# Edge loop of a graph-attention layer: a third PSUM buffer, one-bank softmax with key rows from DRAM, sums one place later, and values and counts in rows of 33

## The chip, the cores and the metric

The kernel runs on one core of one Trainium2 chip. The metric is the device time of one execution in microseconds (us). The granted clock is the share of TensorE's full 2.4 GHz that the records show. The engines are called PE (TensorE; PEld its weight loads), DVE (VectorE), ACT (ScalarE), POOL (GpSimd) and SP (the sync engine, which here only issues DMAs).

## The reference

`x` is 6,250 nodes of 256 features; there are 106,250 edges, sorted by their target `dst`, each with 256 features of its own. Eight heads of 32.

```python
x = x + gnn(layernorm(x), src, dst, edge_attr)      # first part
    q, k, v = x @ Wq + bq, x @ Wk + bk, x @ Wv + bv ; e = edge_attr @ We
    alpha = (q[dst] * (k[src] + e)).sum(head) / sqrt(32)          # per edge and head
    ea    = exp(alpha - segment_max(alpha, dst)[dst])
    out   = segment_sum((v[src] + e) * ea / segment_sum(ea, dst)[dst], dst) + x @ Ws + bs
x = x + ffn(layernorm(x))                            # second part: top 2 of 8 experts, 256 -> 512 -> 256
```

## The kernel before

Three phases follow one another. The first projects 49 tiles of 128 nodes to q, k, v and the skip term, writes a table of v and k rows to DRAM and prepares the tables of the edge loop. The second, the edge loop (lines 678 to 1162), is what the change is about. The third adds the skip term, normalises again and runs the experts.

**Items and chunks.** The edges are cut into 880 items of 128 edges (one per partition), each item belonging to one tile of 128 target nodes. Sixteen items are a chunk, so there are 55 chunks. A place is a step of a chunk, 0 to 15. The loop is written out in full: every engine runs its own list of steps, made by `plan`, and semaphores with credits (`counters`) keep the lists in step.

**One item.** PE turns the 128x256 edge features (`ps_t`, L960), ACT copies them to `aT` (L905), PE multiplies by `We` into the left half of a PSUM buffer `ps_e` (L976) and gathers the q rows into its right half by a one-hot matmul (L980). POOL has gathered the v and k rows of the edges' sources by an indirect DMA into `kv_ring` (L818, four slots). DVE adds e to both (L1059), reduces the item before over the heads (L1047) and multiplies k+e by q (L1065). There are two `ps_e` buffers: `project` of item i waits until DVE has multiplied item i-2.

**The softmax of a chunk, one chunk behind.** The 16 x 8 scores of a chunk lie side by side as 128 columns. POOL masks them (`am`, L835), PE turns them (`scores`, L1010), so that a partition is an (item, head) pair and DVE can scan along the edges for each target's running minimum, forwards and backwards (L1075, L1079). A target whose edges go on in the next item needs minima across partitions: PE spreads each partition's first and last key as rows (`keys`, L1004 to L1006), ACT makes "not the same key" distances from them (L926, L927), PE spreads the minima (L1014 to L1016), and DVE takes two fused add-and-minimum passes (`own`, L1084, L1088). DVE then forms and subtracts the least value (L1094 to L1101), PE turns the result back and forms the rescaling exponent (`turn_scores`, L1020 to L1023), and ACT exponentiates (L942 into the eight count columns of `ve_ke`, L945 into `factor`), which releases `ea_ready`.

**Weighing and summing, up to two chunks behind.** POOL multiplies the 256 values of an item by their eight weights (`weigh`, L828), ACT makes a one-hot of the targets (`select`, L883, L887), PE sums by target (L1029 into one of two `ps_u` buffers) and DVE adds the sum to the node tile's slot (L1135). At the start of a chunk DVE rescales the slot in use by `factor` (L1113 for 256 values, L1114 for 8 counts). `LAG` says how many places behind the scores each of these runs: weigh 15 (POOL runs about four places ahead of DVE), select 11, sum and add 13.

**SP** issues, in one list, the loads of edge features (`a_ring`, four slots), of target rows (`loc_c`) and of the chunk's tables (`run_c`, `resets`, `tab_c`). In the first phase it issues the stores of each node tile, and ahead of tile 43's stores a block of first loads for the edge loop (`edge_loop_inputs`).

Of the kernel before, what the change touches and what calls it, by code (L numbers as in the profile page):

```python
# [6 lines left out]
F32 = mybir.dt.float32  # L7
# [7 lines left out]
P = 128  # L15
# [6 lines left out]
N_KV = 4  # L22
N_A = 4
# [8 lines left out]
def gnn_ffn(nc, x, src, dst, edge_attr, Wq, bq, Wk, bk, Wv, bv, We, Ws, bs, Wg, bg, gbias, W1, b1, W2, b2, out):  # L32
# [23 lines left out]
    with ExitStack() as ctx:  # L56
# [29 lines left out]
        reset_table = dram("reset_table", (IT, P))  # L86
        loc_table = dram("loc_table", (NCH * CH // SEL, SEL * P), BF16)
# [26 lines left out]
        values, counts = node_slots[:, 0:NT, 0:D], node_slots[:, 0:NT, D:UW]  # L114
# [17 lines left out]
        run_c = [sb(f"run_c{i}", [P, P], F32, c_soft) for i in range(2)]  # L132
        resets = [sb(f"resets{i}", [P, P + 1], F32, c_soft) for i in range(2)]
# [3 lines left out]
        reset_loaded = [sem(f"reset_loaded{i}", c_soft) for i in range(2)]  # L137
        loc_loaded = [sem(f"loc_loaded{i}", c_soft) for i in range(NLOC)]
# [13 lines left out]
        with ExitStack() as c1:  # L152
# [21 lines left out]
            head_i = sb1("head_i", [P, 1], I32)  # L174
            stepped = sb1("stepped", [NT, IT])
# [54 lines left out]
            tables_written = sem("tables_written", c1)  # L230
            resets_ready = sem("resets_ready", c1)
# [29 lines left out]
            def _(sp):  # L261
# [26 lines left out]

                def to_table(table, tile):
                    sp.dma_start(table[0:nf * P, :].rearrange("(b p) e -> p b e", p=P), tile[:, 0:nf, :]).then_inc(tables_written, 16)  # L290
                    if n_last:
                        sp.dma_start(table[nf * P:IT, :], tile[0:n_last, nf, :]).then_inc(tables_written, 16)

                def edge_loop_inputs():
# [4 lines left out]
                    sp.wait_ge(tables_written, 16 * (1 + 3 * (2 if n_last else 1)))  # L299
                    sp.dma_start(tab_c[:, 0, :, :].rearrange("p t i -> p (t i)"), tab_table[:, 0:3 * CH]).then_inc(tab_loaded[0], 16)  # L300
                    sp.dma_start(run_c[0][:, :], run_table[0:CH, :][:, None, :].to_broadcast([CH, H, P])).then_inc(run_loaded[0], 16)
                    sp.dma_start(resets[0][:, 0:P], reset_table[0:CH, :][:, None, :].to_broadcast([CH, H, P])).then_inc(reset_loaded[0], 16)
                    for n in range(NLOC - 1):
                        sp.dma_start(loc_c[n][:, :], loc_table[n:n + 1, :].to_broadcast([P, SEL * P])).then_inc(loc_loaded[n], 16)

                for j in range(NT):
# [8 lines left out]
                    if j == LOCS_OUT:  # L315
                        sp.wait_ge(tables_ready, LOCS)
# [10 lines left out]
                sp.wait_ge(tables_written, 16 * (1 + 3 * (2 if n_last else 1)))  # L327
# [126 lines left out]
            def _(dve):  # L454
# [223 lines left out]
        with ExitStack() as c3:  # L678
# [12 lines left out]
            ve_ke = sb3("ve_ke", [P, 2 * CH + 2, UW])  # L691
            sel = sb3("sel", [P, N_W, P])
# [5 lines left out]
            key_prev = sb3("key_prev", [P, 1])  # L698
# [9 lines left out]
            ps_e = [ps3(f"ps_e{i}", [P, 512]) for i in range(2)]  # L708
# [3 lines left out]
            ps_a, ps_k = ps_ak[:, 0:P], ps_ak[:, P:P + KW]  # L712
            ps_r, ps_x, ps_d = ps_rx[:, 0:KW], ps_rx[:, KW:KW + P], ps_rx[:, KW + P:KW + P + H]


            s, at, grant = counters(c3, a_turned=N_A, aT_ready=2, e_ready=2, ve_added=N_KV, kq_ready=2,
                                    alpha_ready=0, apart_ready=0, sel_ready=0, apartT_ready=0, selT_ready=0, weighted=2 * CH, summed=2 * CH, acc_added=2,

                                    am_ready=0, run_by_head=0, keyed=0, keys_apart=0, key_kept=0, offs_ready=0,
                                    scores_turned=0, scanned_f=0, scanned=0, min_spread=0, owned_f=0, owned=0, least1_ready=0,  # L720
                                    least_ready=0, shifted_ready=0, shifted_turned=1, ea_ready=0, rescaled=2, values_rescaled=0,
# [47 lines left out]
            def _(sp):  # L769
# [13 lines left out]
                def load(c, par, steps):  # L783
                    for kind, i, back in steps:
# [7 lines left out]
                        if i == 0 and c > 0:  # L792
# [4 lines left out]
                                         ).then_inc(reset_loaded[par], 16)  # L797
                        if c * CH + i < N_A:
# [8 lines left out]
            def _(pool):  # L807
# [14 lines left out]
                def weigh(c, par, i):  # L822
# [4 lines left out]
                    ve = by_head(ve_ke[:, par * CH + i, 0:D], C)  # L827
                    g.tensor_tensor(ve, ve, ve_ke[:, par * CH + i, D:UW][:, :, None].to_broadcast([P, H, C]),  # L828
# [27 lines left out]
            def _(act):  # L856
# [40 lines left out]
                def emit(c, par, steps):  # L897
                    for kind, i, back in steps:
# [19 lines left out]
                        elif kind == "apart":  # L918
# [3 lines left out]
                            act.wait_ge(s["keyed"], at("keyed", c - 1))  # L922
# [3 lines left out]
                            nc.scalar.activation(not_f[:, :], ps_k, ACT.Abs, scale=-1.0, bias=run[:, 0:1])  # L926
                            nc.scalar.activation(not_l[:, :], ps_k, ACT.Abs, scale=-1.0, bias=run[:, P - 1:P]).then_inc(s["keys_apart"], 1)  # L927
                            nc.scalar.copy(key_prev[:, :], run[:, P - 1:P]).then_inc(s["key_kept"], 1)
# [7 lines left out]
                        elif kind == "exp":  # L936
# [5 lines left out]
                            nc.scalar.activation(ve_ke[:, (1 - par) * CH:(2 - par) * CH, D:UW], by_head(ps_x, H), ACT.Exp, scale=-SCALE)  # L942
# [5 lines left out]
                over_chunks(act, emit, what="select", parts={3: "apart", 4: "offs", 11: "exp"})  # L948

            @block.tensor  # L950
            def _(pe):
# [18 lines left out]
                def project(c, i, n):  # L970
                    pe.wait_ge(s["aT_ready"], at("aT_ready", c * CH + i))

                    pe.wait_ge(s["ve_added"], at("ve_added", c * CH + (i - 2)))
                    pe.wait_ge(s["kq_ready"], at("kq_ready", c * CH + (i - 2)))
# [828 lines left out]
```

## Time and profile before

| | |
|---|---|
| median of 3 runs | 2530.81 us (2526.67 to 2532.15) |
| the profiled execution, its time | 2519.88 us |
| its span, first to last instruction | 2518.1 us |
| first phase | to about 222 us |
| edge loop: first and last matmul with `We` begin | 227.5 us, 1903.5 us |
| mean granted TensorE clock | 0.967; 1.00 from 500 to 1500 us |

Busy time counts overlapping records of an engine once. The ends of matmuls are modelled, so a stall of PE shorter than a matmul's modelled tail doesn't show as idle time; it shows as a longer distance between starts.

### The profile page before, as it was taken

The page shows a single profiled execution, that of the slowest core. Times are in us where ns is not written, and L with a number is a line of the kernel's source. Part 1 is how long each engine was busy: PE and PEld are TensorE (multiplying, and loading weights), DVE is VectorE, ACT ScalarE, POOL GpSimd, SP SyncE. Part 2 cuts the span into 40 slices and gives each one's busy share as a digit, 9 for nine tenths or more (in the row PEclk, how much of TensorE's full clock was granted, in tenths as well). Part 3 has the DMA queues.
Part 4 walks back from the last instruction along what each step waited for, and adds up shares of the span by engine and source line. Part 5 has one row for each costly group of instructions (what it writes and reads, how often), then busy time and mean ns, then how long its engine had stood idle before and what let it go on. Part 6 is the DMA issues. An engine that isn't in the chain of part 4 may idle for free. (4 is left out here: it accounts for less than half of the span.)

```text
span 2518.1 us, 62222 instructions
## 1 busy us (share of the span) xinstructions
PE 2368.8 (94%) x13314; PEld 1994.0 (79%) x13315; DVE 1990.4 (79%) x5253; ACT 1573.8 (62%) x4349; POOL 1809.0 (72%) x2137
## 2 busy tenths in 40 slices
PE   6998999999999999999999999999995658999998
PEld 2445888888888888888888888888883647999998
DVE  6875999999999999999999999999997872222222
ACT  1122677777777777777777777777774125666665
POOL 4223788888888888888888888888886205666666
PEclk9999999999999999999999999999998558999999
DMA  7325877788788778778877777777772672433443
GB/s 230 129 107 182 243 230 229 227 233 232 225 232 228 222 231 232 230 230 232 233 230 229 232 223 231 233 226 227 232 229 81 193 224 53 71 63 63 69 67 54
DMA packets 337730, 476.37 MB, mean 189 GB/s; under 512 B 61382, under 2 KB 268556, under 8 KB 337116
## 3 DMA queue, kind: packets, MB, share of 16 engines
q0 software_dynamic: 92576, 259.72, 39.2%
q1 hardware_dynamic: 238556, 213.23, 27.7%
q8 instruction: 102, 1.67, 0.3%
q14 instruction: 208, 1.70, 0.2%
q10 hardware_dynamic: 6288, 0.05, 0.2%
HBM read 425.40 MB, written 50.57 MB: 189 GB/s over the span
## 5 line engine op out<-in xcount | busy, mean ns | idle before, releaser
L818 POOL DMA_INDIRECT kv_ring<-vk_table,tab_c x880 | 859.7, 977 | 250.9 <-issue 168.2
L976 PE MATMUL ps_e<-we_sb,aT 128*128 128x256 f32 x3520 | 916.4, 383 | 12.3 <-DVE ve_ke L1065 7.8
L976 PEld LDWEIGHTS ps_e<-we_sb,aT 128*128 128x128 f32 x3520 | 600.6, 191 | 82.7 <-issue 31.3
L1059 DVE TENSOR_TENSOR ve_ke<-kv_ring,ps_e 128x512 f32<-128x512 f32 x880 | 601.4, 683 | 47.9 <-PE ps_e L980 17.9
L828 POOL TENSOR_TENSOR ve_ke<-ve_ke 128x256 f32<-128x256 f32 x880 | 551.2, 630 | 16.9 <-ACT factor L945 3.3
L1029 PE MATMUL ps_u<-ve_ke,sel 128*128 128x264 f32 x1760 | 544.3, 391 | 10.1 <-DVE node_slots L1135 5.6
L980 PE MATMUL ps_e<-q_slots,selT 128*128 x1760 | 517.2, 375 | 0.0
L905 ACT COPY aT<-ps_t 128x256 f32<-128x256 f32 x880 | 325.4, 370 | 283.6 <-PE ps_t L960 246.9
L1135 DVE TENSOR_TENSOR node_slots<-node_slots,ps_u 128x264 f32 x880 | 369.9, 420 | 29.0 <-PE ps_u L1029 25.0
L980 PEld LDWEIGHTS ps_e<-q_slots,selT 128*128 128x128 f32 x1760 | 334.7, 190 | 45.6
L1047 DVE TENSOR_REDUCE alpha<-ve_ke 128x8 f32<-128x256 f32 x880 | 362.9, 412 | 2.0
L1065 DVE TENSOR_TENSOR ve_ke<-ve_ke,ps_e 128x256 f32<-128x256 f32 x880 | 361.6, 411 | 1.9
L883 ACT ACTIVATE apart<-iota_free,tab_c 128x128 f32<-128x128 f32 x880 | 348.2, 396 | 3.5 <-PE ps_u L1029 3.2
L960 PE MATMUL ps_t<-ident,a_ring 128*128 128x128 f32 x1760 | 336.4, 273 | 7.1 <-issue 7.1
L887 ACT ACTIVATE sel<-apart 128x128 f32<-128x128 f32 x880 | 272.9, 310 | 105.4 <-ACT apart L883 2.8
L960 PEld LDWEIGHTS ps_t<-ident,a_ring 128*128 128x128 f32 x1760 | 247.0, 141 | 105.3 <-issue 8.1
L1029 PEld LDWEIGHTS ps_u<-ve_ke,sel 128*128 128x128 f32 x1760 | 270.0, 190 | 32.9 <-POOL ve_ke L828 22.6
L1764 DVE TENSOR_TENSOR y_full<-ps_y,b_sb 128x256 f32<-128x256 f32 x112 | 47.6, 425 | 278.4 <-PE ps_y L1733 278.4
L1725 PE MATMUL ps_h<-tT,w_now 128*128 128x128 f32 x1792 | 219.6, 276 | 0.0
L1641 POOL DMA_INDIRECT t_in<-xn_table,take_i x112 | 111.0, 991 | 149.9 <-DVE gate_of L1760 88.6
L1733 PE MATMUL ps_y<-w_sb,hT 128*128 x896 | 212.0, 379 | 0.0
L1725 PEld LDWEIGHTS ps_h<-tT,w_now 128*128 128x128 f32 x1792 | 210.3, 193 | 0.1
(255 smaller groups left out, 2631.3 us busy)
## 6 DMA issues: line engine op xcount, KB each, us to landing
a_ring<-in_edge_attr SPq DMA_DIRECT2D x880, 128.0 KB
loc_c<-loc_table SPq DMA_DIRECT2D x220, 128.0 KB, 3.9
kv_ring<-vk_table,tab_c POOLq DMA_INDIRECT x880
vk_table<-kv_out SPq DMA_DIRECT2D x49, 256.0 KB, 2.0
skip_table<-skip_out SPq DMA_DIRECT2D x49, 128.0 KB, 1.7
skip<-skip_table SPq DMA_DIRECT2D x7, 896.0 KB, 9.5
xn_table<-node_slots SPq DMA_DIRECT2D x7, 896.0 KB, 5.1
w_sb<-in_L_ffn_W SPq DMA_DIRECT2D x2, 2048.0 KB, 10.1
```

Of the source, the lines that this page charges most:

```text
L818: g.indirect_dma_start(out=kv_ring[:, i % N_KV, :], out_offset=None, in_=vk_table, in_offset=bass.IndirectOffsetOnAxis(ap=tab_c[:, c % N_T ...
L828: g.tensor_tensor(ve, ve, ve_ke[:, par * CH + i, D:UW][:, :, None].to_broadcast([P, H, C]), ALU.mult).then_inc(s["weighted"], 1)
L883: nc.scalar.activation(apart[i % 2][:, :], iota_free[:, :], ACT.Abs, scale=-1.0, bias=tab_c[:, c % N_TAB, 1, i:i + 1]).then_inc(s["apart_r ...
L960: last = t.transpose(ps_t[i % 2][:, k * P:(k + 1) * P], a_ring[:, i % N_A, k * P:(k + 1) * P], ident[:, :])
L976: t.matmul(ps_e[i % 2][:, 0:D], aT[i % 2][:, k * P:(k + 1) * P], we_sb[:, k, :], start=(k == 0), stop=(k == KD - 1))
L980: last = t.matmul(ps_e[i % 2][:, D:2 * D], selT[i // SEL % 2][:, i % SEL * P:(i % SEL + 1) * P], q_moving[part][:, bass.ds(n * SLOT, D)], ...
L1029: t.matmul(ps_u[i % 2][:, 0:UW], sel[:, i % N_W, :], ve_ke[:, (par + back) % 2 * CH + i, :], start=True, stop=True).then_inc(s["summed"], 1)
L1047: v.tensor_reduce(alpha[par][:, i * H:(i + 1) * H], by_head(ve_ke[:, 2 * CH + i % 2, 0:D], C), AX_X, ALU.add).then_inc(s["alpha_ready"], 1)
L1059: v.tensor_tensor(ve_ke[:, to:ke + 1:ke - to, 0:D], kv.rearrange("p (t d) -> p t d", t=2), e[:, None, :].to_broadcast([P, 2, D]), ALU.add) ...
L1065: v.tensor_tensor(ve_ke[:, ke, 0:D], ve_ke[:, ke, 0:D], ps_e[i % 2][:, D:2 * D], ALU.mult).then_inc(s["kq_ready"], 1)
L1135: v.tensor_tensor(to, sofar, ps_u[i % 2][:, 0:UW], ALU.add).then_inc(s["acc_added"], 1)
L1725: last = t.matmul(ps_h[par][:, f * P:(f + 1) * P], w1_now[par][:, k, f * P:(f + 1) * P], tT[par][:, k * P:(k + 1) * P], start=(k == 0), st ...
```

## The change

1. **Three `ps_e` buffers** in place of two (`N_E = 3`, buffer by item number modulo 3): `project` of item i waits for DVE's item i-3.
2. **The softmax in one bank.** `ps_ak` and `ps_rx` become `ps_s`: the turned scores (and later, in the same columns, the turned-back result), the spread minima, and the exponent. The third `ps_e` takes the bank that this frees.
3. **Key rows from DRAM.** The three spreading transposes of `keys`, and ACT's copy of the key carried to the next chunk, go away. The first phase writes two tables of keys (five more DMA issues at tile 9, rows of 32 bytes), and SP loads two rows per chunk, spread over the partitions (two more DMAs per chunk).
4. **One spread minimum by 8 columns**: the transpose of the carried minimum (L1014) becomes a matmul of 8 columns.
5. **Places.** sum and add 14, select 12; PE's scores at place 4 (was 3), minima 7 (6), turn_scores 12 (10); ACT's exp 13 (11). DVE's `least` is split over places 7 and 8, the subtraction moves from 8 to 9.
6. **Rows of 33.** `ve_ke` and the node slots hold, for each head, 32 values and then the count, where they held 256 values and then 8 counts. Every operation on values or counts now goes through rows of 32 at a pitch of 33; the rescaling is one operation over 264.

```diff
+N_E = 3
-        values, counts = node_slots[:, 0:NT, 0:D], node_slots[:, 0:NT, D:UW]
+        by_tile = node_slots[:, 0:NT, 0:UW].rearrange("p j (h w) -> p j h w", w=C + 1)
+        sums, counts = by_tile[:, :, :, 0:C], by_tile[:, :, :, C]
...
+            def load_keys(sp, c):
+                keys = key_c[c % 2]
+                sp.dma_start(keys[:, 0:P], first_table[c * CH:(c + 1) * CH, :].rearrange("(o i) h -> o (i h)", o=1).to_broadcast([P, P])
+                             ).then_inc(key_loaded[c % 2], 16)
+                sp.dma_start(keys[:, P:KW], last_table[c * CH:(c + 1) * CH + 1, :].rearrange("(o i) h -> o (i h)", o=1).to_broadcast([P, P + H])
+                             ).then_inc(key_loaded[c % 2], 16)
...
+                def keys_to_tables():
+                    sp.wait_ge(keys_ready, 3)
+                    sp.dma_start(last_table[0:1, :], no_key[:, :]).then_inc(tables_written, 16)
+                    for k, table in enumerate((first_table[0:IT, :], last_table[1:IT + 1, :])):
+                        sp.dma_start(table[0:nf * P, :].rearrange("(b p) h -> p b h", p=P), keys_io[:, k, 0:nf, :]).then_inc(tables_written, 16)
+                        if n_last:
+                            sp.dma_start(table[nf * P:IT, :], keys_io[0:n_last, k, nf, :]).then_inc(tables_written, 16)
...   # edge_loop_inputs
+                    load_keys(sp, 0)
...   # SP, place 0 of each chunk, after run_c and resets
+                            if c >= 2:
+                                sp.wait_ge(s["keys_apart"], at("keys_apart", c - 2))
+                            load_keys(sp, c)
...
+            ve_heads = ve_ke[:, :, :].rearrange("p s (h w) -> p s h w", w=C + 1)
-            ps_ak = ps3("ps_ak", [P, 512])
-            ps_rx = ps3("ps_rx", [P, 512])
+            ps_s = ps3("ps_s", [P, 512])
+            ps_a, ps_r, ps_d = ps_s[:, 0:P], ps_s[:, P:P + KW], ps_s[:, P + KW:P + KW + H]
+            ps_x = ps_a
...
-                       select=FIRST_WEIGH,
-                       sum=FIRST_WEIGH + 2,
-                       add=FIRST_WEIGH + 2)
+                       select=FIRST_WEIGH + 1,
+                       sum=FIRST_WEIGH + 3,
+                       add=FIRST_WEIGH + 3)
...   # POOL
-                    ve = by_head(ve_ke[:, par * CH + i, 0:D], C)
-                    g.tensor_tensor(ve, ve, ve_ke[:, par * CH + i, D:UW][:, :, None].to_broadcast([P, H, C]),
+                    ve = ve_heads[:, par * CH + i, :, 0:C]
+                    g.tensor_tensor(ve, ve, ve_heads[:, par * CH + i, :, C:C + 1].to_broadcast([P, H, C]),
...   # ACT
-                            act.wait_ge(s["keyed"], at("keyed", c - 1))
+                            act.wait_ge(key_loaded[1 - par], 32 * ((c - 1) // 2 + 1))
-                            nc.scalar.copy(key_prev[:, :], run[:, P - 1:P]).then_inc(s["key_kept"], 1)
-                over_chunks(act, emit, what="select", parts={3: "apart", 4: "offs", 11: "exp"})
+                over_chunks(act, emit, what="select", parts={3: "apart", 4: "offs", 13: "exp"})
...   # PE
-                    pe.wait_ge(s["kq_ready"], at("kq_ready", c * CH + (i - 2)))
+                    pe.wait_ge(s["kq_ready"], at("kq_ready", c * CH + (i - N_E)))
-                        elif kind == "keys":
...
-                            t.transpose(ps_r[:, KW - P:KW], min_l[par][:, 0:1].to_broadcast([P, P]), ident[:, :])
+                            t.matmul(ps_r[:, P:P + H], min_l[par][:, 0:1].to_broadcast([P, P]), ident[:, P - H:P], start=True, stop=True)
-                over_chunks(pe, emit, what="sum", parts={0: "keys", 3: "scores", 6: "minima", 10: "turn_scores"})
+                over_chunks(pe, emit, what="sum", parts={4: "scores", 7: "minima", 12: "turn_scores"})
...   # DVE
-                    v.tensor_tensor(ve_ke[:, to:ke + 1:ke - to, 0:D], kv.rearrange("p (t d) -> p t d", t=2),
-                                    e[:, None, :].to_broadcast([P, 2, D]), ALU.add).then_inc(s["ve_added"], 1)
+                    v.tensor_tensor(ve_heads[:, to:ke + 1:ke - to, :, 0:C], kv.rearrange("p (t h c) -> p t h c", t=2, c=C),
+                                    by_head(e, C)[:, None, :, :].to_broadcast([P, 2, H, C]), ALU.add).then_inc(s["ve_added"], 1)
...
-                    v.tensor_tensor(a, a, factor[:, :, None].to_broadcast([P, H, C]), ALU.mult).then_inc(s["values_rescaled"], 1)
-                    v.tensor_tensor(held, held, factor[:, :], ALU.mult).then_inc(s["rescaled"], 1)
+                    v.tensor_tensor(a, a, factor[:, :, None].to_broadcast([P, H, C + 1]), ALU.mult).then_inc(s["rescaled"], 1)
-                over_chunks(dve, emit, what="add", parts={3: "scan", 4: "scan_back", 6: "own", 7: "least", 8: "shift"})
+                over_chunks(dve, emit, what="add", parts={3: "scan", 4: "scan_back", 6: "own",
+                                                         7: "least_first", 8: "least_last", 9: "shift"})
```

## Rows read from the trace of the kernel before

**Rows 1.** The page, busy time, share of the span and instructions of each engine.

```profile
PE 2368.8 (94%) x13314; PEld 1994.0 (79%) x13315; DVE 1990.4 (79%) x5253; ACT 1573.8 (62%) x4349; POOL 1809.0 (72%) x2137
```

**Rows 2.** Windows: busy us of each engine, clock, DMA share, GB/s, inside the loop.

```profile
500.00:1000.00 500.00, 494.84 (x2810) 427.32 (x2809) 477.84 (x1225) 362.97 (x1050) 425.57 (x541) 1.00 0.80 229
```

**Rows 3.** Line L976 alone: durations in ns, first and last start.

```profile
L976 PE MATMUL ps_e<-we_sb,aT x3520: 378/379/797, 227.5 to 1903.5; 128*128 128x256 f32 x196
```

**Rows 4.** Timeline of PE over one chunk: start us, us, instruction.

```profile
988.55 0.27 PE L1004 MATMUL ps_ak<-ident,key_prev 128*128 128x128 f32 x1
...
988.87 0.61 PE L1029 MATMUL ps_u<-ve_ke,sel 128*128 128x264 f32 x2
...
991.30 1.03 PE L976 MATMUL ps_e<-we_sb,aT 128*128 128x256 f32 x4
...
993.07 1.03 PE L976 MATMUL ps_e<-we_sb,aT 128*128 128x256 f32 x4
...
994.40 0.71 PE L1029 MATMUL ps_u<-ve_ke,sel 128*128 128x264 f32 x2
...
995.17 1.03 PE L976 MATMUL ps_e<-we_sb,aT 128*128 128x256 f32 x4
...
1004.34 1.03 PE L976 MATMUL ps_e<-we_sb,aT 128*128 128x256 f32 x4
...
1006.32 1.10 PE L976 MATMUL ps_e<-we_sb,aT 128*128 128x256 f32 x4
...
1007.50 0.28 PE L1020 MATMUL ps_rx<-ident,min_f 128*128 128x8 f32 x2
...
1008.01 0.61 PE L1029 MATMUL ps_u<-ve_ke,sel 128*128 128x264 f32 x2
...
1017.99 0.45 PE L976 MATMUL ps_e<-we_sb,aT 128*128 128x256 f32 x1 [0.32 <-DVE ve_ke L1065]
```

**Rows 5.** Timeline of DVE, same chunk, places 8 to 10.

```profile
1005.77 0.41 DVE L1065 TENSOR_TENSOR ve_ke<-ve_ke,ps_e 128x256 f32<-128x256 f32 x1
...
1006.63 0.68 DVE L1059 TENSOR_TENSOR ve_ke<-kv_ring,ps_e 128x512 f32<-128x512 f32 x1
...
1008.23 0.68 DVE L1059 TENSOR_TENSOR ve_ke<-kv_ring,ps_e 128x512 f32<-128x512 f32 x1
```

**Rows 6.** Timeline of POOL, same chunk.

```profile
993.37 0.41 POOL L835 TENSOR_TENSOR am<-tab_c,alpha 128x128 f32<-128x128 f32 x1
993.74 1.18 POOL L828 TENSOR_TENSOR ve_ke<-ve_ke 128x256 f32<-128x256 f32 x2
...
998.71 0.98 POOL L818 DMA_INDIRECT kv_ring<-vk_table,tab_c  x1 [0.16 <-issue]
...
1000.49 0.98 POOL L818 DMA_INDIRECT kv_ring<-vk_table,tab_c  x1 [0.16 <-issue]
...
1010.86 0.63 POOL L828 TENSOR_TENSOR ve_ke<-ve_ke 128x256 f32<-128x256 f32 x1
```

**Rows 7.** Timeline of ACT, same chunk: the exponent that releases the weighing.

```profile
1008.47 0.26 ACT L945 ACTIVATE factor<-ps_rx,carried 128x8 f32<-128x8 f32 x1
```

**Rows 8.** Waits from 300 to 1900 us, PE's longest and SP's longest: us, times, longest.

```profile
PE ps_e L976 <- DVE ve_ke L1065: 5.5, 21, 0.7
...
SPq L802 <- PE ps_t L960: 487.7, 790, 3.7
```

**Rows 9.** Single lines: operations on rows with gaps (min/median/max ns); the counts' rescaling.

```profile
L559 DVE TENSOR_TENSOR tab<-t_rep,ii_i x1: 1061/1061/1061, 110.9 to 110.9; 128x880 f32<-128x880 f32 x1
L360 POOL TENSOR_TENSOR dst_sb<-run_g x1: 1665/1665/1665, 53.1 to 53.1; 128x889 f32<-128x889 f32 x1
L1114 DVE TENSOR_TENSOR node_slots<-node_slots,factor 128x8 f32 x55 | 11.5, 209 | 0.0
```

**Rows 10.** Timeline of SP and DVE at the end of the first phase.

```profile
203.15 0.62 SPq L301 DMA_DIRECT2D run_c<-run_table  x1
...
210.09 0.69 DVE L615 TENSOR_TENSOR kv_out<-ps_p,b 128x512 f32<-128x512 f32 x1 [5.40 <-DMA skip_table<-skip_out]
```

More of the change, by code:

```diff
@@ L113, in gnn_ffn @@
         x_sb = node_slots[:, 1:NT + 1, D:2 * D]
-        values, counts = node_slots[:, 0:NT, 0:D], node_slots[:, 0:NT, D:UW]
+        values = node_slots[:, 0:NT, 0:D]
+        by_tile = node_slots[:, 0:NT, 0:UW].rearrange("p j (h w) -> p j h w", w=C + 1)
+        sums, counts = by_tile[:, :, :, 0:C], by_tile[:, :, :, C]
         x1 = node_slots[:, 0:NT, UW:SLOT]
@@ L132, in gnn_ffn @@
         run_c = [sb(f"run_c{i}", [P, P], F32, c_soft) for i in range(2)]
+        KW = 2 * P + H
+        key_c = [sb(f"key_c{i}", [P, KW], F32, c_soft) for i in range(2)]
         resets = [sb(f"resets{i}", [P, P + 1], F32, c_soft) for i in range(2)]
@@ L137, in gnn_ffn @@
         reset_loaded = [sem(f"reset_loaded{i}", c_soft) for i in range(2)]
+        key_loaded = [sem(f"key_loaded{i}", c_soft) for i in range(2)]
         loc_loaded = [sem(f"loc_loaded{i}", c_soft) for i in range(NLOC)]
@@ L315, in _ @@
                     if j == LOCS_OUT:
+                        with nc.allow_non_contiguous_dma(reason="eight head keys of an item"):
+                            keys_to_tables()
                         sp.wait_ge(tables_ready, LOCS)
@@ L521, in floats @@
                         v.tensor_scalar(run_f, run_g[:, :, :], BIG, None, ALU.mult).then_inc(tables_ready, 1)
-                    else:
+                        v.memset(no_key[:, :], -BIG).then_inc(keys_ready, 1)
+                        then(v.tensor_scalar(head_row[:, :], iota_free[:, 0:H], BIG / H, None, ALU.mult))
+                    else:
+                        for k, e in enumerate((0, P - 1)):
+                            v.tensor_tensor(keys_io[:, k, :, :], run_f[:, :, e:e + 1].to_broadcast([P, IB, H]),
+                                            head_row[:, None, :].to_broadcast([P, IB, H]), ALU.add).then_inc(keys_ready, 1)
                         dve.wait_ge(gathered[1], 16 * IB)
@@ L925, in emit @@
                             act.sem_inc(s["act_pace"], 1)
-                            nc.scalar.activation(not_f[:, :], ps_k, ACT.Abs, scale=-1.0, bias=run[:, 0:1])
-                            nc.scalar.activation(not_l[:, :], ps_k, ACT.Abs, scale=-1.0, bias=run[:, P - 1:P]).then_inc(s["keys_apart"], 1)
-                            nc.scalar.copy(key_prev[:, :], run[:, P - 1:P]).then_inc(s["key_kept"], 1)
+                            nc.scalar.activation(not_f[:, :], key_c[1 - par][:, :], ACT.Abs, scale=-1.0, bias=run[:, 0:1])
+                            nc.scalar.activation(not_l[:, :], key_c[1 - par][:, :], ACT.Abs, scale=-1.0, bias=run[:, P - 1:P]
+                                                 ).then_inc(s["keys_apart"], 1)
                         elif kind == "offs":
@@ L941, in emit @@
                             act.sem_inc(s["act_pace"], 1)
-                            nc.scalar.activation(ve_ke[:, (1 - par) * CH:(2 - par) * CH, D:UW], by_head(ps_x, H), ACT.Exp, scale=-SCALE)
+                            nc.scalar.activation(ve_heads[:, (1 - par) * CH:(2 - par) * CH, :, C], by_head(ps_x, H), ACT.Exp, scale=-SCALE)
                             act.wait_ge(s["rescaled"], at("rescaled", c - 2))
@@ L979, in project @@
                     for part in range(2):
-                        last = t.matmul(ps_e[i % 2][:, D:2 * D], selT[i // SEL % 2][:, i % SEL * P:(i % SEL + 1) * P],
+                        last = t.matmul(ps_e[(c * CH + i) % N_E][:, D:2 * D], selT[i // SEL % 2][:, i % SEL * P:(i % SEL + 1) * P],
                                         q_moving[part][:, bass.ds(n * SLOT, D)], start=(part == 0), stop=(part == 1))
@@ L998, in emit @@
                                 next_tiles[:] = node_tiles_of(c + 1)
[L999 to L1006 removed]
                         elif kind == "scores":
                             pe.wait_ge(s["am_ready"], at("am_ready", c - 1))
[L1009 removed]
+                            pe.wait_ge(s["ea_ready"], at("ea_ready", c - 2))
                             t.transpose(ps_a, am[:, :], ident[:, :]).then_inc(s["scores_turned"], 1)
@@ L1089, in softmax @@
                                                op1=ALU.min, accum_out=min_l[1 - par][:, :]).then_inc(s["owned"], 1)
-                    elif part == "least":
+                    elif part == "least_first":
                         dve.wait_ge(s["offs_ready"], at("offs_ready", c - 1))
@@ L1095, in softmax @@
                                                op0=ALU.add, op1=ALU.min).then_inc(s["least1_ready"], 1)
+                    elif part == "least_last":
                         dve.wait_ge(s["least1_ready"], at("least1_ready", c - 1))
@@ L1261, in _ @@
                 for j, n in groups:
-                    nc.gpsimd.tensor_tensor(by_heads(x1[:, j:j + n, :]), by_heads(values[:, j:j + n, :]),
+                    nc.gpsimd.tensor_tensor(by_heads(x1[:, j:j + n, :]), sums[:, j:j + n, :, :],
                                             inv[:, j:j + n, :][:, :, :, None].to_broadcast([P, n, H, C]), ALU.mult).then_inc(att_ready, 1)
```

56 lines of the change are left out of this document (24 added, 32 removed).

## The prediction

> **What bounds the kernel now.** I read the page first, for the engines' shares of the whole span [rows 1], then the windows, for the stage that the change touches. From 500 to 1000 us PE is busy 99% of the time at full clock, DVE 95.6% and POOL 85% [rows 2]. So PE is the first suspect, with DVE right behind it. The reader is to see that busy time doesn't settle it: a PE record carries a modelled tail, so a short stall hides in it. The list of waits has PE waiting little: its longest entry is 5.5 us of 1600 [rows 8]. Starts of the same instruction tell more, so the third view is L976 alone: 880 items take from 227.5 to 1903.5 us, 1.906 us an item, 30.5 us a chunk of 16 [rows 3].
>
> The fourth view is PE's timeline over one chunk. An undisturbed place takes 993.07 - 991.30 = 1.77 us [rows 4], and 16 of them 28.3 us. The softmax's own PE work comes on top: three spreading transposes take 988.87 - 988.55 = 0.32 us, so 0.11 each; the turned scores 0.11; the three of `minima`, by the same price, 0.33; `turn_scores` 1008.01 - 1007.50 = 0.51 [rows 4]. Together 1.27, and 29.6 with the items. The other 30.5 - 29.6 = 0.9 us of a chunk is PE standing still, in short stalls.
>
> Where? Place 3 takes 995.17 - 993.07 = 2.10: 0.33 over 1.77, of which the scores explain 0.11. The sum starts at 994.40; half of POOL's pair of weighings that starts at 993.74 and takes 1.18 ends at about 994.33 [rows 4, 6]. PE waits for the item that POOL's mask has delayed. Place 9 takes 1006.32 - 1004.34 = 1.98, 0.21 too much: `project` of item 10 waits for DVE's L1065 of item 8, which starts at 1005.77 and takes 0.41, so ends at 1006.18 [rows 4, 5]. DVE was late because of the softmax passes at places 6 to 8. The wrap to the next chunk ends the same way: 0.32 us idle, released by L1065 [rows 4].
>
> The other engines' need of a chunk decides what can be won. DVE's undisturbed place takes 1008.23 - 1006.63 = 1.60 [rows 5]; with softmax and rescaling its busy share gives 0.956 x 30.5 = 29.1 us. POOL's place takes 1000.49 - 998.71 = 1.78, and the mask 993.74 - 993.37 = 0.37 more [rows 6]: 16 x 1.78 + 0.37 = 28.9 us. Three engines need 29.6, 29.1 and 28.9 us, and their coupling makes 30.5 of it.
>
> **The change, part by part.**
>
> *PE's instructions.* Dropping `keys` takes away 0.32 us. The carried minimum as an 8-column matmul is two passes for one transpose: `turn_scores` is four such passes and a transpose in 0.51, 0.10 each [rows 4], so it adds about 0.1 (between 0, if passes overlap as in a tail, and 0.11). Net -0.22 us a chunk; PE's need becomes 29.6 - 0.22 = 29.4 us.
>
> *PE's stalls, 0.9 us a chunk.* With three buffers, `project` of item 10 waits for item 7, which DVE multiplied a whole place (1.6 to 1.8 us) earlier than item 8; the 0.21 at place 9 and the 0.32 at the wrap are far under that, and go. With sums at lag 14 and the weighing still at 15, the item that the mask delays is wanted one place later, 1.77 us against a delay of 0.22; it goes too. What should stay are the irregular delays of whole chunks, and new small ones, since PE will lead DVE by only 29.4 against 29.1. I take two thirds of the 0.9, 0.6 us; the bounds are none of it and all of it.
>
> *DVE.* The rescaling loses the counts' operation, mean 0.209 us [rows 9], but it lay in the first one's completion time, so between 0 and 0.2 us. Splitting `least` fills a short wait; at most 0.1. Nothing is added to its loop.
>
> *Rows of 33.* The trace has no row with rows of 32 at a pitch of 33. The nearest on DVE writes rows of 16 at a pitch of 48: 880 elements in 1061 ns, 1.21 ns each with all overhead [rows 9], where the flat L1059 takes 0.68 us for 512, 1.33 each [rows 5]. So 0. On POOL the nearest has rows of 127 at a pitch of 128: 889 elements in 1665 ns, 1.87 ns each [rows 9], against 0.63 us for 256, 2.46 each, in the weighing [rows 6]. So 0 as well, but there the rows are long and only seven, and POOL has little room: 30.5 - 28.9 = 1.6 us a chunk, 0.1 us on each weighing of 0.63. That is the bound from above that turns the sign, and the rival below.
>
> *The moved steps.* `turn_scores` goes from place 10 to 12, 2 x 1.77 = 3.5 us later, and with it the exponent, for which POOL's first weighing waits, with every later gather behind it in POOL's list. Now the exponent ends at 1008.47 + 0.26 = 1008.73 and that weighing starts at 1010.86 [rows 6, 7]: 2.1 us of cover, so POOL would wait 1.4 us. PE wants the result one place (1.77 us) later than now, so PE has no loss from it; POOL loses 1.4 us only if it doesn't get them back where it now waits for DVE (30.5 - 28.9 = 1.6 us a chunk in all). I take 0, and 1.4 us as the bound. ACT waits at exp as now, for the same distance from `turn_scores`. DVE's subtraction one place later frees `run_c` a place later for SP, which then issues four loads of up to 0.62 us [rows 10] ahead of an edge-feature load; SP waits 487.7 us in 790 waits, 0.6 each [rows 8], and `a_ring` is four items, 7 us, deep. So 0.
>
> *Key loads.* Two rows of about 512 bytes to 128 partitions are 0.13 MB a chunk; at 229 GB/s a chunk moves 7.0 MB [rows 2], so 2% more on a DMA share of 0.80. Hidden. ACT's key copy goes; ACT is busy 73% [rows 2], so 0.
>
> *Once.* In the first phase the block of first loads on SP already makes DVE wait 5.40 us for a store [rows 10]; two more issues of up to 0.62 us each lengthen it by 1.2 us. The five table writes at tile 9, at the same price, are 3 us of SP between stores; SP has that much idle, so 0 to 3; I take 0.3. Together 1.5 us.
>
> *Sum.* 0.22 + 0.6 = 0.82 us on 54 full chunks is 44 us, less 1.5: 42 us. The profiled execution would go from 2519.88 to 2478 us. It lies 11 us below the median of the runs shown, 2530.81; on that scale the forecast is **2489 us**. The bounds of this case: with every stall gone, (0.22 + 0.9) x 54 - 1.5 = 59 us off, 2472; with half of the 0.6, (0.22 + 0.3) x 54 - 1.5 = 27 off, 2504.
>
> **The rivals.** *The wait only moves.* PE's `sum` still waits, through two `ps_u` buffers, for DVE's addition two items back. If PE's lead now ends there, or DVE waits at `scan` for scores that PE turns one place later, a chunk takes perhaps 30.1 us. For it: DVE's 29.1 leaves 0.3 us to PE's 29.4. Against: today no wait for an addition is long enough to head PE's list [rows 8], and DVE's peak of softmax work (places 6 to 8) is what the third buffer bridges. 0.4 x 54 - 1.5 = 20 us off: 2511.
>
> *The late exponent holds POOL.* If POOL can't use its slack elsewhere, its chunk is 28.9 + 1.4 = 30.3, and the change does next to nothing: 0.2 x 54 - 1.5 = 9 us off, 2522. Against it: the 1.6 us of present slack is larger than 1.4.
>
> *POOL pays for the rows: slower.* The weighing's 2.46 ns an element lie 0.59 above the 1.87 of the operation on long rows [rows 6, 9]. If that is what its factor, read anew every 32nd element, costs it, and gaps in the values' rows cost the same again, a weighing takes 256 x 0.59 ns = 0.15 us more, a chunk 28.9 + 16 x 0.15 = 31.3, and the loop (31.3 - 30.5) x 54 = 43 us more: 2575. It decides from 0.1 us a weighing, 16%, on. Against it: the difference may as well be an operation's fixed cost, which weighs more on 256 elements than on 889. The Trainium skill (GPSIMD Engine Reference, section Performance pitfalls for Q7 kernels) states that reads with a step over 8 bytes cost POOL about half as much again, and that it is the inner step that counts. Read so, it doesn't reach this operation, whose inner steps are 4 bytes and 0; if it did, an estimate by that page makes a weighing 0.95 us and the loop 189 us longer. No run here shows its price.
>
> **How the numbers follow.** Stalls mostly gone, 0.64; the wait only moves, 0.18; late exponent or nothing, 0.10; rows cost POOL or DVE, 0.08. For 8 in 10 the range takes the first two whole, with the 11 us between profile and median as play: 2466 to 2520. The measurement can tell about 0.2%, 5 us. Faster: 0.64 + 0.18 + 0.05 of the third case, 0.87; the same 0.05; slower 0.08.
>
> **What would show it.** Right: L976's starts span about 1676 - 44 = 1632 us; places 3 and 9 take 1.77 in PE's timeline (place 4 has the 0.11 of the scores); L828 stays at 0.62 to 0.63 and L1059 at 0.68; DVE's busy share rises to 98%; POOL's first weighing waits for ACT. Wrong: a longer L828; PE's starts 1.9 apart with `acc_added` as releaser; DVE idle at the scan; or a chunk that POOL's wait for the exponent sets.

## The result, and the profile after

The changed kernel takes 2536.8 us (median of 10 executions, 2533.6 to 2543.5) against 2527.7 us of the kernel before on the same chip (10, 2525.3 to 2533.1): ratio 1.0038, 95% interval 1.0030 to 1.0045. It is slightly slower, by more than measurement play. The forecast was 2489 us. The profiled execution took 2536.19 us, its span 2534.3.

The page's busy line and the window inside the loop, in the columns of [rows 1, 2]:

```profile
PE 2366.8 (93%) x13204; PEld 1993.9 (79%) x13205; DVE 1975.2 (78%) x5201; ACT 1570.8 (62%) x4294; POOL 1812.8 (72%) x2137
500.00:1000.00 500.00, 489.87 (x2752) 423.86 (x2751) 465.41 (x1195) 357.62 (x1020) 422.47 (x535) 1.00 0.79 232
```

PE and DVE do *less* of a window than before: no engine became full. `project`'s first matmul, now L1013, answers to [rows 3]:

```profile
L1013 PE MATMUL ps_e<-we_sb,aT x3520: 379/379/792, 230.6 to 1916.2; 128*128 128x256 f32 x196
```

It starts 3.1 us later than before and takes 1685.6 us instead of 1676, so a chunk of 16 is 1685.6 / 879 x 16 = 30.68 us against 30.51. In the chunk that starts at 1182.50 us the stalls named at place 3 and at the wrap are gone, that at place 9 is smaller (1.85 us against 1.98), and others stand in their place: places 1, 2, 6 and 8 take 1.96 to 2.02 us. The waits from 300 to 1900 us (us, times, longest), and below them SP's own queue:

```profile
POOL ve_ke L865 <- ACT factor L982: 48.1, 49, 1.3
PE ps_u L1057 <- DVE node_slots L1161: 15.3, 30, 2.5
PEld ps_t L997 <- DMA a_ring<-in_edge_attr: 5.1, 10, 1.2
...
SPq L839 <- PE ps_t L997: 370.1, 554, 3.7
SPq L828 <- DVEq L1132: 49.9, 52, 1.1
```

Two are new and come once a chunk: POOL's first weighing waits 1 us for the exponents, and SP's load of the run rows waits 1 us for DVE's shift. The timelines of one chunk show the first (DVE, PE, ACT, POOL in turn):

```profile
1016.89 0.28 DVE L1131 TENSOR_TENSOR least<-ps_s,least 128x128 f32<-128x128 f32 x1
...
1019.85 0.31 PE L1051 MATMUL ps_s<-ident,least 128*128 128x128 f32 x1
...
1020.28 0.41 ACT L979 ACTIVATE ve_ke<-ps_s 128x128 f32<-128x128 f32 x1 [0.70 <-PE ps_s L1051]
1020.47 0.24 ACT L982 ACTIVATE factor<-ps_s,carried 128x8 f32<-128x8 f32 x1
...
1018.89 0.97 POOL L855 DMA_INDIRECT kv_ring<-vk_table,tab_c  x1 [0.16 <-issue]
1020.90 0.62 POOL L865 TENSOR_TENSOR ve_ke<-ve_ke 128x256 f32<-128x256 f32 x1 [1.03 <-ACT factor L982]
1021.66 0.99 POOL L855 DMA_INDIRECT kv_ring<-vk_table,tab_c  x1
```

The shift has ended at 1017.17, but PE turns it at 1019.85, by its place in the list; the exponents end at 1020.71 and POOL, idle for 1.03 us, goes on at 1020.90. The gather behind it starts at 1021.66, 2.77 us after the one before; a place is 1.78 us [rows 6]. In [rows 6, 7] this weighing had 2.1 us to spare.

### The profile page after: what moved, and what is told of

The parts are those of the page before. It is cut to its first block and busy times, and to the rows that moved or that the text cites. A ratio compares the mean times of both kernels' runs of the same rounds, so it can differ in the third digit from the quotient of the medians.

```text
span 2534.3 us, 61900 instructions
## 1 busy us (share of the span) xinstructions
PE 2366.8 (93%) x13204; PEld 1993.9 (79%) x13205; DVE 1975.2 (78%) x5201; ACT 1570.8 (62%) x4294; POOL 1812.8 (72%) x2137
## 5 line engine op out<-in xcount | busy, mean ns | idle before, releaser
L1013 PE MATMUL ps_e<-we_sb,aT 128*128 128x256 f32 x3520 | 908.7, 381 | 2.0 <-ACT aT L942 1.3
L1087 DVE TENSOR_TENSOR ve_ke<-kv_ring,ps_e 128x512 f32<-128x512 f32 x880 | 600.1, 682 | 74.1 <-PE ps_e L1017 31.7
L1013 PEld LDWEIGHTS ps_e<-we_sb,aT 128*128 128x128 f32 x3520 | 601.7, 191 | 49.3 <-ACT aT L942 2.9
L1057 PE MATMUL ps_u<-ve_ke,sel 128*128 128x264 f32 x1760 | 561.0, 401 | 32.6 <-DVE node_slots L1161 20.9
L1161 DVE TENSOR_TENSOR node_slots<-node_slots,ps_u 128x264 f32 x880 | 370.2, 421 | 29.2 <-DVE node_slots L1141 15.5
```

The lines of the kernel that those rows point to most:

```text
L1013: t.matmul(ps_e[(c * CH + i) % N_E][:, 0:D], aT[i % 2][:, k * P:(k + 1) * P], we_sb[:, k, :], start=(k == 0), stop=(k == KD - 1))
L1057: t.matmul(ps_u[i % 2][:, 0:UW], sel[:, i % N_W, :], ve_ke[:, (par + back) % 2 * CH + i, :], start=True, stop=True).then_inc(s["summed"], 1)
L1087: v.tensor_tensor(ve_heads[:, to:ke + 1:ke - to, :, 0:C], kv.rearrange("p (t h c) -> p t h c", t=2, c=C), by_head(e, C)[:, None, :, :].to_ ...
L1161: v.tensor_tensor(to, sofar, ps_u[i % 2][:, 0:UW], ALU.add).then_inc(s["acc_added"], 1)
```

## The experiments

Three theories. A: the late exponents hold POOL, which paces the loop. B: the third buffer only moves PE's wait to the additions. C: the new operations themselves cost time. All ratios are to the kernel before on the same chip, with 95% intervals.

**The step one place earlier (e1).**

```diff
-parts={4: "scores", 7: "minima", 12: "turn_scores"}     # PE
+parts={4: "scores", 7: "minima", 11: "turn_scores"}
-parts={3: "apart", 4: "offs", 13: "exp"}                # ACT
+parts={3: "apart", 4: "offs", 12: "exp"}
```

> The changed kernel with one edit: TensorE turns the scores back at place 11 instead of 12 and ScalarE takes the exponents at place 12 instead of 13. In the changed kernel POOL's first weighing of a chunk waits about 1 us for the exponents, and VectorE's last subtraction ends 2.3 us before TensorE turns the scores, so the edit should add no wait on TensorE. Theory A (the late exponents hold POOL, which then issues the gathers late): the wait of 1 us goes, a chunk falls from 30.67 us to 29.7 or less, so 2480 to 2490 us. Theory B (the third buffer only moves TensorE's wait to the sums' two PSUM buffers): POOL's wait goes but the chunk stays, 2525 to 2540 us. Theory C (the longer backward scan, the exponents written at a step of 33, the key rows' transfers): unchanged, 2533 to 2540 us.

2504.1 us, ratio 0.9927 (0.9914 to 0.9941): two numbers in the list are worth 1.1%, 28 us. POOL's wait for the exponents is gone but for one. Starts of L1013 in its span and in chunks 25 to 27:

```profile
L1013 PE MATMUL ps_e<-we_sb,aT x3520: 379/379/792, 230.3 to 1883.9; 128*128 128x256 f32 x196
...
979.23 1.03 PE L1013 MATMUL ps_e<-we_sb,aT 128*128 128x256 f32 x4
...
1008.89 0.81 PE L1013 MATMUL ps_e<-we_sb,aT 128*128 128x256 f32 x3
...
1038.54 0.81 PE L1013 MATMUL ps_e<-we_sb,aT 128*128 128x256 f32 x3
```

Undisturbed chunks take 29.66 and 29.65 us, but the mean is 1653.6 / 879 x 16 = 30.10: A is right in kind, its 2480 to 2490 us too low.

**The step one place later (e2).**

```diff
-12: "turn_scores"      -13: "exp"
+13: "turn_scores"      +14: "exp"
```

> The changed kernel with the same step moved the other way: scores turned back at place 13, exponents at place 14. One place is 1.9 us. Theory A: POOL waits 1.9 us more in each of 54 chunks, so 2610 to 2640 us. Theories B and C: 2533 to 2550 us, as POOL's wait would be slack that other waits take up.

2600.4 us, 1.0298 (1.0284 to 1.0311). POOL's wait:

```profile
POOL ve_ke L865 <- ACT factor L982: 121.4, 48, 2.9
```

It is 121.4 / 48 = 2.5 us a chunk instead of 1.0, and the time rises by 65 us, 1.2 us a chunk. B and C are out as the main cause. A's dose is a little off (1.5 us of wait for a place of 1.8), and the time lies 10 us below its range.

**POOL's order alone (e5).** In the changed kernel, exponents at 13:

```diff
+if kind == "weigh" and i == 0 and held is not None:
+    gather(c, par, held)
+    held = None
 if kind == "weigh":
     weigh(...)
```

> The changed kernel (scores turned back at 12, exponents at 13) with one edit on POOL alone: the gather of place 15, which stood behind the first weighing of a chunk, is issued ahead of it. The exponents come no earlier, but POOL spends its wait for them on a gather of 0.98 us that it has to issue anyway. Theory A (POOL, some 29.3 us of work a chunk, paces the loop and the wait of 1 us lengthens it): most of the wait is filled, so about as fast as the run with the step one place earlier, 2500 to 2512 us. A rival: the late exponents cost through another engine (ScalarE's order, TensorE's sums): no gain, 2530 to 2540 us.

2512.1 us, 0.9961 (0.9948 to 0.9975). The exponents are as late as before the edit, yet filling the wait with one gather gives back 0.8%. So it was in the main POOL's lost time that counted, not the lateness for anyone else; some 9 us remain to e1.

**Two buffers, old places and lag (e3).**

```diff
-N_E = 3
+N_E = 2
-select=FIRST_WEIGH + 1, sum=FIRST_WEIGH + 3, add=FIRST_WEIGH + 3
+select=FIRST_WEIGH, sum=FIRST_WEIGH + 2, add=FIRST_WEIGH + 2
-4: "scores", 7: "minima", 12: "turn_scores"     # PE; ACT's exp 13
+3: "scores", 6: "minima", 10: "turn_scores"     # ACT's exp 11
-7: "least_first", 8: "least_last", 9: "shift"   # DVE
+7: "least", 8: "shift"
```

> The changed kernel with two PSUM buffers for the projection instead of three, and with the places and the lag of the kernel before (scores 3, minima 6, scores turned back 10, exponents 11, both least steps at 7, shift 8, sums at lag 13). Left of the change are the key rows from DRAM, the one bank and the rows of 33 with one rescaling. Theory C (these cost time): slower than the kernel before by 5 to 20 us, 2535 to 2550 us. Theory A and theory B: the rest costs next to nothing, so the kernel before's time within 0.4%, less 5 us for the transposes that TensorE no longer makes: 2518 to 2532 us.

2527.1 us, 1.0006 (0.9997 to 1.0015). Key rows by transfer, the carried minimum by 8 columns, one bank, rows of 33 and one rescaling add up to nothing that can be measured, and they gain nothing either, though PE makes three transposes less. That a cost and a gain among them cancel is not excluded by this run.

**Three buffers, old places (e4).** The last four lines of e3's diff alone; `N_E = 3` and lag 14 stay.

> The changed kernel with three buffers and lag 14, and with the places of the kernel before (scores 3, minima 6, scores turned back 10, exponents 11, both least steps at 7, shift 8). Theory A: POOL's wait for the exponents goes, but TensorE, one place further ahead of VectorE, may wait up to 1 us for the mask, the scan or the shift: 2485 to 2515 us. Theory B: 2525 to 2540 us. Theory C: 2533 us or more.

2525.3 us, 1.0003 (0.9994 to 1.0011). The buffer (with the lag, but without the places) is worth nothing: PE now runs into the mask.

```profile
PEld ps_s L1039 <- POOL am L872: 32.5, 52, 3.2
PE ps_s L1039 <- POOL am L872: 21.4, 48, 3.0
```

Its weight loads wait 32.5 us there, 0.6 us a chunk (the matmul's wait is mostly the same time). With PE an item further ahead of DVE, its softmax steps had to move one place; the change moved the turned scores by two.

**The buffer undone (e12).** e1 with

```diff
-N_E = 3
+N_E = 2
```

> The run with scores turned back at 11 and exponents at 12, with two PSUM buffers for the projection instead of three. Theory A: TensorE is one place closer behind VectorE, so the exponents come one place (1.8 us) later for POOL than with three, and POOL waits 1 us or more for them: 2530 to 2570 us; the third buffer earns its time only together with the places. If the places alone made the gain: 2500 to 2510 us.

2549.8 us, 1.0094 (1.0078 to 1.0109). So the places need the buffer as the buffer needs the places. The number was forecast, the reason was not: POOL has no wait for the exponents here; PE waits for DVE's products and DVE for PE's scores.

```profile
PE ps_e L1013 <- DVE ve_ke L1093: 26.5, 72, 1.8
DVE scan_f L1103 <- PE ps_s L1039: 22.8, 49, 1.5
```

**The lag undone (e7).** e1 with the third and fourth line of e3's diff (sums and additions at lag 13).

> The run with scores turned back at 11 and exponents at 12, with the lags of the kernel before (sums and additions at 13, selections at 11). The weighed rows and the additions must be ready one place (1.8 us) sooner. Theory A says that POOL's weighing of item 0 starts right after the exponents at about TensorE's place 12 and ends 0.9 us on, so that a sum at place 13 would wait for it, and later sums for VectorE's additions: 0.3 to 1 us a chunk, 2515 to 2560 us. If the lag is worth nothing: 2500 to 2508 us.

2556.9 us, 1.0123 (1.0108 to 1.0138), within the range given. PE waits for POOL's weighings, some 1 us each time (weight loads and matmuls, mostly the same time):

```profile
PEld ps_u L1057 <- POOL ve_ke L865: 61.2, 59, 3.7
PE ps_u L1057 <- POOL ve_ke L865: 46.8, 50, 3.5
```

**PE's saved work put back (e11).** e1 with three transposes at place 0.

```diff
+elif kind == "keys":
+    pe.wait_ge(s["owned"], at("owned", c - 2))
+    for at_column in (KW - P, 0, P):
+        t.transpose(ps_r[:, at_column:at_column + P], min_l[par][:, 0:1].to_broadcast([P, P]), ident[:, :])
```

> The run with scores turned back at 11 and exponents at 12, with three transposes added on TensorE at place 0, as large as those of the key rows that the change removed (their result is not read). If TensorE is the bound there (an undisturbed chunk of 29.66 us): 0.3 us a chunk, 16 us more, 2515 to 2523 us. If POOL or VectorE paces it still: 0 to 5 us more, 2502 to 2509 us.

2519.4 us, 0.9978 (0.9969 to 0.9987): 13 us more than e1 by the ratios (the two medians, from two chips, are 15 apart), within the range given. An undisturbed chunk takes 30.00 us, 0.34 over e1's:

```profile
709.77 1.03 PE L1013 MATMUL ps_e<-we_sb,aT 128*128 128x256 f32 x4
...
739.77 1.03 PE L1013 MATMUL ps_e<-we_sb,aT 128*128 128x256 f32 x4
```

That is the whole price of three transposes (0.32 in [rows 4]), so PE is the bound in e1's undisturbed chunks, and most of e1's gain of 18 us on the kernel before is the dropped transposes, which e3 with its two buffers could not turn into time.

**Chunk 0's key rows later (e6).** e1 with

```diff
 sp.dma_start(resets[0]...)
-load_keys(sp, 0)
...
 # behind the loop over the node tiles
+load_keys(sp, 0)
 sp.wait_ge(stored[0], 16 + 32 * ceil_div(NT, 2))
```

> The run with scores turned back at 11 and exponents at 12, with chunk 0's key rows loaded after the last node tile's store instead of within SP's block of loads at tile 43 of the first phase. In the changed kernels that block is 1.0 us longer, VectorE waits 6.3 us there instead of 5.4, TensorE idles longer and its granted clock falls to 0.58 of full for some 4 us, and the edge loop starts 2.8 us later. If the block is the cause, the loop starts at 227.5 us again and the clock stays at full: 2.5 to 3 us less, 2500 to 2502 us. If it is not (the stores of the key tables at tile 9, say): the loop still starts at 230 us, 2503 to 2505 us.

2505.7 us, 0.9934 (0.9921 to 0.9947), in neither range and not told apart from e1 as a whole. In the first phase the trace decides. Windows 210 to 214 and 214 to 218 us of the kernel before, then e1, then e6 (columns as [rows 2]):

```profile
210.00:214.00 4.00, 1.84 (x6) 1.05 (x7) 3.60 (x9) 1.18 (x3) 0.85 (x2) 1.00 0.44 162
214.00:218.00 4.00, 4.00 (x10) 1.71 (x9) 1.69 (x4) 0.41 (x1) 0.60 (x1) 1.00 0.25 88
```
```profile
210.00:214.00 4.00, 0.80 (x5) 0.54 (x5) 2.84 (x7) 0.71 (x2) 0.73 (x1) 0.99 0.61 226
214.00:218.00 4.00, 4.00 (x7) 1.67 (x6) 0.76 (x3) 0.47 (x2) 0.73 (x1) 0.58 0.30 107
```
```profile
210.00:214.00 4.00, 1.62 (x6) 0.83 (x6) 3.37 (x9) 0.85 (x3) 0.73 (x1) 1.00 0.40 146
214.00:218.00 4.00, 4.00 (x10) 1.73 (x10) 1.55 (x5) 0.33 (x1) 0.73 (x1) 1.00 0.27 98
```

In e1 PE stood idle for longer in the first window (busy 0.80 us, against 1.84 and 1.62), and its granted clock fell to 0.58 in the second, for the most part the lower level of 1.2 GHz; the loop starts at 230.3 us. In e6 it stays at 1.00, 2.4 GHz, and the loop starts at 228.0 (227.5 before). So 1 us of SP's issues became 2.3 to 2.8 us of loop start.

**Key rows loaded twice (e8).** e1 with

```diff
-keys = key_c[c % 2]
+for keys in (key_x[c % 2], key_c[c % 2]):
     ... both loads, as before
```

> The run with scores turned back at 11 and exponents at 12, in which SP loads each chunk's key rows twice, once into a spare tile, in every chunk: two more transfers, 132 KB, and about 1 us more of SP's time a chunk. Its undisturbed chunk is 29.66 us and its mean 30.1, as gathers and edge rows sometimes land late. Theory C (the key rows' transfers make those land late): the mean rises by the same 0.1 to 0.4 us a chunk that one pair would cost, so 2508 to 2527 us. If the key rows' transfers cost nothing in the loop: 2502 to 2507 us, the first phase's 1 to 2 us included.

2584.5 us, 1.0232 (1.0218 to 1.0247): 77 us more than e1 by the ratios, over three times the most that any theory gave. **The same with SP's block at place 4 (e10):**

```diff
-if i == 0 and c > 0:      # SP: softmax_done, run_c, resets, load_keys
+if i == 4 and c > 0:
```

> The run that loads the key rows twice (2584 us), with SP's block of a chunk at place 4 instead of place 0. Queue theory: what cost 80 us was the order on SP, where the block stands ahead of the edge row that TensorE turns at place 15, so 2500 to 2512 us. Bandwidth theory: the 132 KB more a chunk on the DMA engines cost it, so 2560 us or more.

2584.2 us, 1.0241 (1.0224 to 1.0257). The queue theory as I put it failed: place 0 is nothing special. But the bytes aren't the cause either, by **the second pair moved to place 12 (e13)**, e10 with

```diff
-load_keys(sp, c)
+load_keys(sp, c, (0,))
+if i == 12 and c > 0:
+    load_keys(sp, c, (1,))
```

> The run that loads the key rows twice with SP's block at place 4 (2584 us; TensorE waits for the edge row right behind the block, 141 us in all), with the second pair of transfers at place 12. Burst theory: four key transfers in a row delay the one edge row behind them past its margin, and two pairs apart don't: 2500 to 2515 us. Bandwidth theory: the bytes count, wherever they stand: 2560 us or more.

2513.1 us, 0.9937 (0.9923 to 0.9952), with the same bytes. PE's waits for edge rows in e8, e10 and e13:

```profile
PEld ps_t L998 <- DMA a_ring<-in_edge_attr: 87.8, 52, 3.0
PE ps_t L998 <- DMA a_ring<-in_edge_attr: 66.2, 51, 2.6
```
```profile
PEld ps_t L998 <- DMA a_ring<-in_edge_attr: 80.3, 48, 3.8
PE ps_t L998 <- DMA a_ring<-in_edge_attr: 60.5, 45, 3.4
```
```profile
PEld ps_t L1000 <- DMA a_ring<-in_edge_attr: 5.7, 10, 1.2
PE ps_t L1000 <- DMA a_ring<-in_edge_attr: 1.9, 4, 0.8
```

A burst of six transfers makes the one edge row behind it late, at place 0 and at place 4; SP's timeline of e8 has it:

```profile
1040.47 0.57 SPq L829 DMA_DIRECT2D run_c<-run_table  x1
...
1043.30 1.46 SPq L273 DMA_DIRECT2D key_c<-last_table  x1
1045.51 1.46 SPq L840 DMA_DIRECT2D a_ring<-in_edge_attr  x2
```

Five us pass here from the block's first issue to the edge row's. The median over the chunks between 300 and 1900 us is 4.0 us in e8 and 4.1 in e10, against 3.1 with the four transfers of e1 and e13. Whether SP's extra time to issue them or their bytes ahead of the row make it late is not separated by these runs. With one pair the margin nearly held: 9.2 us of such waits on weight loads in all of e1, and 3.8 on matmuls.

**The fastest versions (e9, e14).** e9 is e6 with e10's diff; e14 is e9 with

```diff
+if i == 12 and c > 0:
     if c >= 2:
         sp.wait_ge(s["keys_apart"], at("keys_apart", c - 2))
     load_keys(sp, c)
```

> The run with chunk 0's key rows loaded late (scores turned back at 11, exponents at 12), and SP's block of a chunk (the wait for the softmax of two chunks before, the run rows, the resets, the two key rows) at place 4 instead of place 0. In the trace that block waits 1 us for VectorE's shift in each chunk and takes 2.2 us, and TensorE then waits 13 us in all for edge rows. If the block holds up the edge rows: those waits go and the time falls by 5 to 13 us, 2492 to 2501 us. If it does not: 2503 to 2508 us.

> The fastest run so far (2499.8 us: scores turned back at 11, exponents at 12, chunk 0's key rows late, SP's block at place 4) with the pair of key rows at place 12 instead of within the block. If the burst of four transfers still makes edge rows late there: 2 to 8 us less, 2492 to 2498 us. If one pair more or less is within the margin: 2498 to 2502 us.

2499.8 us, 0.9899 (0.9884 to 0.9914), and 2499.5 us, 0.9886 (0.9870 to 0.9903). Between e6 and e9 the waits for edge rows fall from 16.7 to 6.5 us in all (weight loads and matmuls) and the time by 9 us by the ratios, as forecast. In e14 PE waits 0.3 us for edge rows in all; the two times are not told apart. Both beat both kernels.

## Why the prediction was wrong, step by step

I forecast 42 us less and measured 9 more (0.38%): 51 us apart. The place of the exponents accounts for 28 of them (e1 against the changed kernel), what e1 still lacks of the forecast for 23.

- *The step that failed is "The moved steps ... I take 0, and 1.4 us as the bound".* The wait was seen and sized (1.4, measured 1.0), and wrongly hidden in POOL's 1.6 us of slack. That slack is a chunk's length less POOL's work; once PE's chunk is to shrink to 29.7 us, it shrinks with it. Undisturbed chunks of the changed kernel take 30.2 to 30.4 us (the two starts below lie 30.39 apart). Some 0.5 us of it POOL waits for DVE's scores in most chunks, which the sum of POOL's places left out (third line: us in all, times, longest):

```profile
1182.50 0.81 PE L1013 MATMUL ps_e<-we_sb,aT 128*128 128x256 f32 x3
...
1212.89 0.81 PE L1013 MATMUL ps_e<-we_sb,aT 128*128 128x256 f32 x3
...
POOL kv_ring L855 <- DVE alpha L1074: 18.3, 34, 1.0
```

  Less the 1.0 us of wait for the exponents, POOL needs 29.2 to 29.4, not 28.9. At the 29.7 that I forecast, 0.3 to 0.5 us of slack were left, too little for the wait. The rival "late exponent holds POOL" gave 30.3 us a chunk, as the undisturbed ones have it (the mean of 30.68 has 0.3 us of irregular delays more); it had 0.10. Undoing the late step is worth 28 us (e1), filling the wait 19 (e5, 0.77%).
- *PE's instructions.* -0.22 was forecast. Three such transposes put back cost 0.3 (e11), and PE's undisturbed chunk in e1 is 29.66 with some 0.4 us of waits in it, so its own work is near 29.3; forecast 29.4.
- *PE's stalls: "I take two thirds of the 0.9, 0.6 us".* Mis-sized, even with the places right. The named ones went, but the rival "the wait only moves" came true in part. PE's timeline in e1, places 8 to 10, and DVE's addition:

```profile
993.87 1.03 PE L1013 MATMUL ps_e<-we_sb,aT 128*128 128x256 f32 x4
994.55 0.43 DVE L1161 TENSOR_TENSOR node_slots<-node_slots,ps_u 128x264 f32 x1
995.12 0.68 PE L1057 MATMUL ps_u<-ve_ke,sel 128*128 128x264 f32 x2
...
995.86 1.03 PE L1013 MATMUL ps_e<-we_sb,aT 128*128 128x256 f32 x4
...
997.71 1.03 PE L1013 MATMUL ps_e<-we_sb,aT 128*128 128x256 f32 x4
```

  At DVE's softmax peak the sum waits for the addition that ends at 994.98; the place takes 1.99 us, the next 1.85, where 1.77 would do. With the one after, some 0.4 us a chunk in all; another 30.10 - 29.66 = 0.44 are irregular delays. So some 0.85 stayed where 0.3 was forecast. With PE's own work 0.1 lower than forecast, e1's mean chunk lies 30.10 - 29.68 = 0.42 us over the forecast, 23 us in 54 chunks.
- *Rows of 33: 0.* Right. POOL's weighing takes 626 ns on average, 630 before, and DVE's L1087 682. The Trainium skill (GPSIMD Engine Reference, Performance pitfalls for Q7 kernels) puts its charge on the inner step; read so, the trace agrees. The rival "POOL pays" is out. ACT's exponents, which the prediction did not price, did take longer (last section), but not on the path.
- *Key loads: hidden.* Right for the bytes (e13), and for one pair nearly so (e14). "`a_ring` is four items, 7 us, deep. So 0" was too easy: SP's margin for one edge row had room for one pair and not for two.
- *Once: 1.5 us.* The loop starts 3.1 us late. The block was 1.0 us longer (1.2 worked out); the fall of the clock behind it was not foreseen (e6).
- DVE's busy share was to rise to 98% and fell to 93%: the bound was another engine. In e1 it is 95.5% from 500 to 1000 us, as before, though the chunk is shorter: DVE is busy for 28.5 us of e1's undisturbed chunks, where 29.1 was taken.

## What to carry to other kernels

Slack is a difference to the loop's present length: when a change is to shorten the loop, take every cover anew at the new length before calling a moved step free. When a buffer lets one engine run an item ahead, its other steps in a hand-written order have to move with it, and here by just that item: the turned scores one place too far cost 28 us, and no step moved at all cost the whole gain. The steps were moved together; which of the others needs its place was not tried. A late producer may cost only because an engine stands idle behind it: work that needs nothing, put ahead of the wait, gives most of it back.

## What the runs showed of the hardware

Exponents written to single columns 132 bytes apart take ACT 408 ns instead of 277 for the same 128 x 128, where eight columns lay together before (the PSUM bank that it reads changed too; no run separates the two). The lines after, and before:

```profile
L979 ACT ACTIVATE ve_ke<-ps_s 128x128 f32<-128x128 f32 x55 | 22.4, 408 | 38.0 <-PE ps_s L1051 38.0
```
```profile
L942 ACT ACTIVATE ve_ke<-ps_rx 128x128 f32<-128x128 f32 x55 | 15.3, 277 | 89.2 <-PE ps_rx L1023 71.0 <-issue 18.2
```

It costs nothing on the path: from the start of this operation to the end of `factor`'s, which releases POOL, pass 0.43 us in the chunk shown above (1020.28 to 1020.71) and 0.44 before (1008.29 to 1008.73).

DVE's backward scan takes 678 ns on average in the changed kernel and 423 before, on the same operands. In the timelines of the changed kernel, then of before, what differs is where POOL's gather stands:

```profile
1006.25 0.99 POOL L855 DMA_INDIRECT kv_ring<-vk_table,tab_c  x1 [0.16 <-DVE ve_ke L1087]
1006.66 0.84 DVE L1107 TENSOR_TENSOR_SCAN scan_b<-resets,scan_f 128x128 f32<-128x128 f32 x1
```
```profile
1027.47 0.98 POOL L818 DMA_INDIRECT kv_ring<-vk_table,tab_c  x1 [0.16 <-issue]
1028.36 0.42 DVE L1079 TENSOR_TENSOR_SCAN scan_b<-resets,scan_f 128x128 f32<-128x128 f32 x1
1028.46 0.72 POOL L828 TENSOR_TENSOR ve_ke<-ve_ke 128x256 f32<-128x256 f32 x1
```

A scan that starts in the middle of a gather ends 0.26 us after the gather; one that starts at its end keeps 0.42. It is so throughout: from 300 to 1900 us of the changed kernel, 36 scans start 0.35 to 0.8 us into a gather, and each ends 0.24 to 0.28 us after it, whether it then takes 0.45 or 0.89 us; five that start earlier in a gather keep 0.42, and five that start in a weighing end 0.3 us after that. The forward scan, which reads one operand from PSUM, takes 0.41 to 0.42 us in all these chunks, though POOL is at work beside it. The Trainium skill (SBUF — State Buffer, Who interferes with whom) says that a DVE instruction with two SBUF inputs contends with a GpSimd instruction that reads SBUF, over a port pair that is an exclusive lock. The scans behind a gather or a weighing agree; in the second timeline the weighing starts inside the scan and is only some 0.09 us longer than its usual 0.63, so it isn't held for the scan's whole 0.32 us that were left. No experiment changes this alone; e1 has it too (583 ns) and is PE-bound all the same.
